# A sandwich transformer block on one core: output projection with doubled adapter and y buffers, low parts ahead of statistics, inverses made early, two pieces moved behind attention

## The reference

```python
x = x + layernorm(attn(layernorm(x)))
x = x + layernorm(ffn(layernorm(x)))
```

## Time and profile before

| | us |
|---|---|
| median of the runs (3) | 1255.57 |
| lowest and highest | 1255.46, 1257.33 |
| the profiled execution's own time | 1251.13 |
| its span, first to last instruction | 1249.4 |
| TensorE busy in the span | 1111.8 (89%) |
| DVE busy | 708.5 (57%) |
| ACT busy | 493.9 (40%) |
| POOL busy | 249.8 (20%) |
| mean granted clock of TensorE | 0.934 of full |

### The profile page before, as it was taken

The page is one execution under the profiler, slowest core; times in us unless marked ns, Lnnn a source line. Parts: engine busy times, 40 slices in busy tenths (PEclk is TensorE's granted clock), DMA queues, the critical chain, the costliest instruction groups (busy, mean ns, idle before and its releaser), DMA issues. The chain is left out here.

```text
span 1249.4 us, 18070 instructions
## 1 busy us (share of the span) xinstructions
PE 1111.8 (89%) x7020; PEld 760.4 (61%) x7020; DVE 708.5 (57%) x983; ACT 493.9 (40%) x1042; POOL 249.8 (20%) x251
## 2 busy tenths in 40 slices
PE   3999999889999999999998975455999999999996
PEld 1877778534455555555553443344888888887884
DVE  4756747777787878877887353354433324324213
ACT  3233233246677777777776431111321111111110
POOL 3525438101311112111111222231000001001001
PEclk9999999687999999999998788676999999999998
DMA  6356686544434445555440433453210200200100
GB/s 238 97 142 176 158 183 172 104 104 78 78 79 79 79 78 101 93 92 95 87 124 24 126 101 109 136 152 118 63 43 1 101 1 9 93 1 17 51 1 34
DMA packets 93417, 113.08 MB, mean 91 GB/s; under 512 B 26260, under 2 KB 54036, under 8 KB 93332
## 3 DMA queue, kind: packets, MB, share of 16 engines
q1 hardware_dynamic: 91476, 108.21, 34.0%
q10 hardware_dynamic: 1856, 3.71, 1.7%
HBM read 68.83 MB, written 42.21 MB: 89 GB/s over the span
## 5 line engine op out<-in xcount | busy, mean ns | idle before, releaser
L828 ACT ACTIVATE prob<-ps_s 128x512 f32<-128x512 f32 (+3 forms) x768 | 323.9, 496 | 185.4 <-PE ps_s L974 178.5
L850 DVE TENSOR_REDUCE neg<-ps_m 128x2 f32<-128x1024 f32 (+2 forms) x224 | 248.2, 1145 | 56.1 <-PE ps_m L939 36.2
L974 PE MATMUL ps_s<-q_op,k_op 50*128 50x512 f32 (+2 forms) x768 | 242.5, 449 | 17.8 <-ACT prob L828 13.2
L939 PE MATMUL ps_m<-k_op,q_op 48*128 48x512 f32 (+2 forms) x768 | 183.5, 416 | 10.5 <-DVE neg L850 6.8
L974 PEld LDWEIGHTS ps_s<-q_op,k_op 50*128 50x128 f32 x768 | 117.5, 192 | 121.5 <-ACT prob L828 60.4
L787 POOL TENSOR_SCALAR_AFFINE_SELECT prob<-prob 128x512 f32<-128x512 f32 x128 | 81.3, 636 | 409.7 <-ACT prob L828 409.7
L988 PE MATMUL ps_y<-prob,vg 128*17 128x512 f32 (+3 forms) x1536 | 153.2, 520 | 0.0
L1504 DVE TENSOR_TENSOR hf<-sl,ps_u 128x512 f32<-128x512 f32 (+1 forms) x44 | 30.2, 687 | 192.0 <-PE ps_u L78 165.5
L850 DVE TENSOR_REDUCE neg_far<-ps_m 128x4 f32<-128x512 f32 (+2 forms) x96 | 100.0, 1048 | 30.1 <-PE ps_m L944 28.6
L1569 PE MATMUL ps_d<-w_high,wp_high 128*128 128x512 f32 (+1 forms) x352 | 115.0, 389 | 0.0
L939 PEld LDWEIGHTS ps_m<-k_op,q_op 48*128 48x128 f32 x768 | 95.9, 196 | 29.0 <-DVE neg L850 20.0
(11 more groups left out here) (164 smaller groups left out, 1683.9 us busy)
## 6 DMA issues: line engine op xcount, KB each, us to landing
y_heads<-y_sb SPq DMA_DIRECT2D x32, 256.0 KB, 2.1
raw<-in_w_ffn SPq DMA_DIRECT2D x31, 256.0 KB, 4.8
k_op<-k_parts SPq DMA_DIRECT2D x28, 256.0 KB, 4.4
q_op<-q_parts SPq DMA_DIRECT2D x56, 128.0 KB, 5.0
v_groups<-v_out SPq DMA_DIRECT2D x16, 272.0 KB, 4.1
x<-in_x SPq DMA_DIRECT2D x4, 1024.0 KB, 7.8
q_parts<-part_h SPq DMA_DIRECT2D x16, 256.0 KB, 2.9
q_parts<-part_l SPq DMA_DIRECT2D x16, 256.0 KB, 2.9
```

What stands on the lines that cost most here:

```text
L828: act.activation(prob[:, v % NPROB, h, unit_cols(u)], ps_s[:, y % NS, unit_cols(u)], ACT.Exp, scale=D ** -0.5).then_inc(s_exp, 1)
L850: nc.vector.tensor_reduce(to[:, :, pairs[0]:pairs[-1] + 1, i - TT * c], scores, axis=AX.X, op=ALU.max, negate=True).then_inc(a_read, 1)
L939: last = nc.tensor.matmul(ps_m[:, g % 2, s, base:base + wide], q_op[buf][r, c, pair, (i - TT * c) * P:(i - TT * c + 1) * P], k_op[buf][r, ...
L974: nc.tensor.matmul(ps_s[:, y % NS, lo:BLK], k_op[buf][r, pair, j * P:(j + 1) * P], q_op[buf][r, c, pair, lo:BLK], start=True, stop=True)\
```

## The change

- The sums are loaded in four DMAs by 256 columns, into a tile of 128 rows; batch 0's in iteration 11 of SP's loop (before: 13), and their inversion stands on DVE behind the last maximum of group 12 (before: behind the last of all). place_inverses(0) moves to iteration 13 (before: end of 14). For batch 1, 28 heads' sums are loaded in iteration 15 and the last four heads' are copied straight out of y_sb.
- ya gets a second buffer, and y a pair of its own for pieces 4 and 5 (y_late).
- In attention, spreads 0 to 2 and projects 0 and 1 stand in earlier slots; project(2) leaves the slots and stands behind attention's last product, and project(3) behind spread(5). finish(1) comes ahead of low(2), finish(2) moves behind attention.
- In stage_project, low(m + 2) and divide(m + 3) come between finish(m) and finish(m + 1). The feed-forward tiles 12 to 19 are split in the feed-forward stage, now three a slice (tiles 12 to 15 are still loaded before), and its first transposes stand beside project(6).
- Feed-forward's PSUM banks are exchanged (ps_g, ps_u with ps_f), and ACT's waits at its start are put at tile 22.

The diff, cut to its core:

```diff
--- before.py
+++ after.py
@@ -37,8 +37,8 @@
+NPB = NP // B
...
-LATE_WEIGHTS = 20
@@ -725,21 +725,26 @@
+            if n == NG - 5:
+                for c in range(HB):
+                    sp.wait_ge(y_out[c], 16 * NHG)
+                tail.load_sums(sp, 0, H)
             if n == NG - 3:
...
-                for c in range(HB):
-                    sp.wait_ge(y_out[c], 16 * NHG)
-                tail.load_sums(sp, 0)
+                tail.place_inverses(sp, 0)
                 tail.load_y(sp, 0)
...
             if n == NG - 1:
+                for c in range(HB):
+                    sp.wait_ge(y_out[c], 16 * (NG - 1))
+                tail.load_sums(sp, 1, H - HG)
                 for i in range(8, 12):
                     tail.load_weights(sp, i)
-                tail.load_ya(sp, 2)
+                tail.load_ya(sp, 3)
                 tail.load_y(sp, 3)
@@ -749,16 +754,18 @@
             if n == NG - 2:
-                tail.place_inverses(sp, 0)
+                sp.wait_ge(pv, NU * (NG - 2))
+                tail.load_ya(sp, 1)
                 for i in range(4, 8):
                     tail.load_weights(sp, i)
-                tail.load_ya(sp, 1)
+                tail.load_ya(sp, 2)
                 tail.load_y(sp, 2)
+        tail.copy_sums(sp, y_sb, 0)
         tail.store_x1(sp, 1)
         tail.load_x(sp, 2)
-        tail.load_ya(sp, 3)
+        tail.load_ya(sp, 4)
         store_y(NG - 1, 1)
-        tail.store_x1(sp, 2)
+        tail.copy_sums(sp, y_sb, 1)
@@ -786,19 +793,19 @@
+                if (n, u) == (NG - 2, 8):
+                    tail.add_adapter(pool, 0)
                 if (n, u) == (NG - 2, 10):
-                    tail.add_adapter(pool, 0)
-                if (n, u) == (NG - 2, 11):
                     tail.add_adapter(pool, 1)
-                if (n, u) == (NG - 1, 3):
+                if (n, u) == (NG - 1, 2):
                     tail.inverse_deviation(pool, 0)
                     tail.residual_pool(pool, 0)
+                if (n, u) == (NG - 1, 3):
                     tail.add_adapter(pool, 2)
                     tail.inverse_deviation(pool, 1)
                     tail.residual_pool(pool, 1)
+                if (n, u) == (NG - 1, 8):
                     tail.add_adapter(pool, 3)
-        tail.inverse_deviation(pool, 2)
-        tail.residual_pool(pool, 2)
@@ -808,7 +815,7 @@
-        highs = {(NG - 2, 11): 0, (NG - 1, 2): 1, (NG - 1, 7): 2, (NG - 1, 10): 3}
+        highs = {(NG - 2, 10): 0, (NG - 1, 0): 1, (NG - 1, 6): 2, (NG - 1, 10): 3}
@@ -886,7 +893,8 @@
-        tail.invert(dve, 0)
+                if entry == (NG - 4, NK - 1):
+                    tail.invert(dve, 0)
@@ -899,22 +907,22 @@
-        weights(NG - 4, range(4))
+        weights(NG - 4, range(2))
+        tail.divide(dve, 0)
+        weights(NG - 4, range(2, 4))
+        tail.divide(dve, 1)
         weights(NG - 3, range(4, 6))
-        tail.divide(dve, 0)
+        tail.low(dve, 0)
         weights(NG - 3, range(6, 8))
-        tail.divide(dve, 1)
-        tail.low(dve, 0)
         tail.low(dve, 1)
         finish(0)
         tail.divide(dve, 2)
         weights(NG - 2, range(8, 10))
+        finish(1)
         tail.low(dve, 2)
-        finish(1)
         tail.divide(dve, 3)
         weights(NG - 2, range(10, 12))
         tail.low(dve, 3)
-        finish(2)
@@ -1011,8 +1019,8 @@
-        for step, m, slot, parts in ((tail.spread, 0, 5, 2), (tail.spread, 1, 8, 2), (tail.project, 0, 14, 4), (tail.spread, 2, 18, 2),
-                                     (tail.project, 1, 20, 4), (tail.spread, 3, 24, 2), (tail.project, 2, 27, 4)):
+        for step, m, slot, parts in ((tail.spread, 0, 2, 2), (tail.spread, 1, 6, 2), (tail.project, 0, 11, 4),
+                                     (tail.spread, 2, 15, 2), (tail.project, 1, 19, 4), (tail.spread, 3, 24, 2)):
...
@@ -1064,14 +1072,16 @@
-            y_in*2 yad_in xr_in over_ps y_div y_sum y_high y_low o_ps
+            y_in*4 yad_in*2 xr_in over_ps y_div y_sum y_high y_low o_ps
...
-        self.y, self.ya, self.xr = room.put("y", [P, 2, CC, W]), room.put("ya_sb", [P, CC, W]), room.put("xr", [P, PT, C])
+        self.y, self.xr = room.put("y", [P, 2, CC, W]), room.put("xr", [P, PT, C])
+        self.ya = [room.put("ya_sb0", [P, CC, W]), nc.alloc_sbuf_tensor_at("ya_sb1", [P, CC, W], F32, offset=start["vg0"])]
+        self.y_late = nc.alloc_sbuf_tensor_at("y_late", [P, 2, CC, W], F32, offset=start["qr"])
@@ -1091,19 +1101,25 @@
+    def y_of(self, m):
...
+        return (self.y_late if m in (NPB, NPB + 1) else self.y)[:, m % 2]
     def load_y(self, sp, m):
+        b, at = m // NPB, slice(m % NPB * W, (m % NPB + 1) * W)
+        if m in (2, 3):
...
+        elif m >= NPB + 2:
+            sp.wait_ge(self.y_low, m - 3)
...
-            sp.dma_start(self.y[:, m % 2, c], self.d["y_heads"][heads_c, 0:D, at]).then_inc(self.y_in[m % 2], 16)
+            sp.dma_start(self.y_of(m)[:, c], self.d["y_heads"][heads_c, 0:D, at]).then_inc(self.y_in[m % NPB], 16)
     def load_ya(self, sp, m):
-        if m:
-            sp.wait_ge(self.y_sum, m)
-        sp.dma_start(self.ya[:], self.d["ya"][b, :, :, at]).then_inc(self.ya_in, 16)
+        b, at = m // NPB, slice(m % NPB * W, (m % NPB + 1) * W)
+        if m >= 2:
+            sp.wait_ge(self.y_sum, m - 1)
+        sp.dma_start(self.ya[m % 2][:], self.d["ya"][b, :, :, at]).then_inc(self.ya_in[m % 2], 16)
@@ -1127,31 +1143,37 @@
-    def load_sums(self, sp, b):
-        if b:
-            sp.wait_ge(self.inv_in, 16 * HB * b)
-        sp.dma_start(self.sums[:], self.d["y_heads"][b * H:(b + 1) * H, D].rearrange("h (k t) -> k h t", k=HB))\
-            .then_inc(self.sums_in, 16)
+    def load_sums(self, sp, b, heads):
...
+        src = self.d["y_heads"][b * H:b * H + heads, D].rearrange("h (k t) -> k h t", k=NPB)
+        for k in range(NPB):
+            sp.dma_start(self.sums[k * H:k * H + heads, b], src[k]).then_inc(self.sums_in, 16)
...
+    def copy_sums(self, sp, y_sb, c):
...
+        for k in range(2):
+            row = (2 * c + k) * H + H - HG
+            sp.dma_start(self.sums[row:row + HG, B - 1], y_sb[D:P:32, c, k * W:(k + 1) * W]).then_inc(self.sums_in, 16)
...
-        for k in range(HB):
-            cols = slice((b * HB + k) * BLK, (b * HB + k + 1) * BLK)
-            sp.dma_start(self.inv[0:H, cols], self.sums[k * H:(k + 1) * H]).then_inc(self.inv_in, 16)
+        for k in range(NPB):
+            sp.dma_start(self.inv[0:H, (b * NPB + k) * W:(b * NPB + k + 1) * W], self.sums[k * H:(k + 1) * H, b])\
+                .then_inc(self.inv_in, 16)
     def invert(self, dve, b):
-        dve.wait_ge(self.sums_in, 16 * (b + 1))
-        self.nc.vector.reciprocal(self.sums[:], self.sums[:]).then_inc(self.inverse, 1)
+        dve.wait_ge(self.sums_in, 16 * (NPB if b == 0 else 3 * NPB))
+        self.nc.vector.reciprocal(self.sums[:, b], self.sums[:, b]).then_inc(self.inverse, 1)
     def divide(self, dve, m):
-        dve.wait_ge(self.y_in[m % 2], 16 * CC * (m // 2 + 1))
+        dve.wait_ge(self.y_in[m % NPB], 16 * CC * (m // NPB + 1))
...
-        self.nc.vector.tensor_tensor(self.y[:, m % 2], self.y[:, m % 2], self.ps_r(m), op=ALU.mult).then_inc(self.y_div, 1)
+        self.nc.vector.tensor_tensor(self.y_of(m), self.y_of(m), self.ps_r(m), op=ALU.mult).then_inc(self.y_div, 1)
...
-        self.nc.vector.tensor_tensor(self.y_l[:, m % 2], self.y[:, m % 2], self.y_h[:, m % 2].bitcast(F32),
+        self.nc.vector.tensor_tensor(self.y_l[:, m % 2], self.y_of(m), self.y_h[:, m % 2].bitcast(F32),
...
@@ -1259,104 +1281,114 @@
         tail.load_y(sp, 4)
-        tail.load_sums(sp, 1)
-        tail.load_x(sp, 3)
         tail.load_y(sp, 5)
-        tail.load_ya(sp, 4)
-        tail.place_inverses(sp, 1)
-        tail.store_x1(sp, 3)
-        tail.load_x(sp, 4)
-        tail.load_weights(sp, 12)
-        tail.load_weights(sp, 13)
         for half in range(2):
             sp.wait_ge(tail.x1_out[half], 16)
         sp.dma_start(tail.x1_first[:], tail.d["x1_blocks"][0]).then_inc(tail.x1_in, 16)
-        for m in last_m:
-            if m + 1 < NP:
-                tail.load_ya(sp, m + 1)
...
+        tail.load_y(sp, 6)
+        tail.load_ya(sp, 5)
+        tail.place_inverses(sp, 1)
+        tail.load_y(sp, 7)
+        for i in range(EARLY_WEIGHTS, EARLY_WEIGHTS + 4):
+            tail.load_weights(sp, i)
+        for m in range(2, NP):
             tail.store_x1(sp, m)
             if m + 1 < NP:
                 tail.load_x(sp, m + 1)
+            if m < NPB:
+                tail.load_ya(sp, m + 4)
     def _(pool):
-        tail.inverse_deviation(pool, 3)
-        tail.add_adapter(pool, 4)
-        tail.residual_pool(pool, 3)
-        for m in last_m:
-            if m + 1 < NP:
-                tail.add_adapter(pool, m + 1)
-            if m == NP - 2:
-                tail.f_inverse_deviation(pool, 0)
+        def finish(m):
...
+        finish(2)
+        tail.add_adapter(pool, 4)
+        tail.add_adapter(pool, 5)
```

(99 more changed lines are left out.)

36 lines of the change are left out of this document (14 added, 22 removed).

## The result

The changed kernel takes 1223.91 us (median of 4 runs, 1219.34 to 1227.31), the kernel before on the same chip 1255.51: ratio 0.9745, 95% interval 0.971 to 0.978. A second comparison of the same kernel (e7) gave 0.9751. It is 32 us faster; 53 were forecast, and 1223.91 lies outside the range of 1191 to 1221. Its profiled execution has a span of 1221.0 us, 28.4 less than before.

The account below looks back on a forecast made before the run. TensorE was taken to bound attention and feed-forward, with a chain of waits between. The terms +7.8 - 13.1 - 46.4 - 1.2 = -52.9 us, from the median 1255.6, gave 1202.7; range 1191 to 1221.

Parts of the forecast that it names:

- Part 5: Feed-forward: splitting eight more tiles there costs 0, less low clock at its start gives -1.2 us.
- A: Rival, 0.13: in attention the sums land as on a free queue, 1199.7; also distance, group 12's last maximum to maxima's end.
- Part 1: Early inversion in attention: DVE waits for the sums, TensorE stands 5.8 us, then low clock 2.0: +7.8 us, bounds +3 and +10.
- D: Rival, 0.04: after the stop TensorE's low clock stays through attention, up to +77, net +19: 1275.
- Part 2: Attention's last two groups: waits and project(2) leave, a wait at project(0) comes: -13.1 us, bounds -17 and -6.
- Part 3: From attention's last result copied (E) to the spreads: they start at E + 16.6, before 20.8; bounds 15.6 and 20.5.
- Part 4: Pieces from the spreads to feed-forward, DVE as the chain: feed-forward starts at E + 60, before 106.4.
- the forecast's case: Whole kernel: the parts as forecast, terms off by a few us, 1202.7; chance 0.62; projects 4 to 7 start 7 to 9 apart.
- B: Rival, 0.11: behind attention pieces keep a pitch of 16, 1233; also distance, maxima's end to attention's last result copied.
- C: Rival, 0.08: feed-forward starved by weight loads, +6, 1209; also distance, attention's last result copied to first spread.

Follow-up runs that it names:

- e7: The changed kernel again, without an edit: ratio 0.9751 to the kernel before.
- e3: Changed kernel with project(0) one slot later in attention, and spread(2) with it: ratio 0.9693 to the kernel before.
- e4: Changed kernel with SP placing batch 1's inverses ahead of x1_first, y of 6 and ya of 5: ratio 0.9651 to the kernel before.
- e9: Changed kernel with low(5) to low(7) each behind the finish of the piece ahead, as before the change: ratio 0.9894 to the kernel before.
- e6: e5's kernel with DVE adding both halves of the residual for pieces 3 to 5 and POOL none: ratio 0.957 to the kernel before.
- e2: Changed kernel with SP issuing the sums' loads ahead of group 14's load, inversion left in place: ratio 0.9643 to the kernel before.
- e5: Changed kernel with e3's and e4's edits and batch 0's inversion moved behind group 13's last maximum: ratio 0.9554 to the kernel before.

## Why the prediction was right, and why it was wrong

The direction was right, and so were the mechanism of each part in the main and the place of the waits for the sums, for low(0) and for the spreads. The collision of DVE with POOL was not foreseen. The size was not right: four terms were too favourable, by 6.0, 9.4, 6.0 and 4.1 us in parts 1 to 4; with 0.4 in Part 5, less the 1.5 that lie ahead of A, that is the difference between the 52.9 forecast and the 28.4 of the profiled execution.

**Part 1: +7.8 forecast, 13.8 measured (12.6 in e7).** The landing (595.0 forecast, 594.08 measured) and the stop (5.8 and 5.82) were right, and so was the rule of the ring order that stood beside them. The step that failed is "half of that is lost: 2.4, of which I take 2.0": it carried the one return to full speed that it had read, 4.9 us behind a wait in front of a project, over to attention as a fixed price. There the return took 3.8 to 12.2 us of nearly unbroken work in five traces with the same stop, and what lies beyond the stop itself cost 8.0 us here and 6.0, 3.8, 1.9 and 4.1 in e7, e3, e4 and e9. So 2.0 was the smallest of what came, met in one trace of five. The row that was nearest had been in hand: 0.60 over 12 us with TensorE busy for 10.5, used for rival D and not for this term. By 12 us at that row's clock the term would have been near 5, and the part 10.5, which is what the first trace had lost when its clock was back; the further 3.3 are the two short falls at 653 and 673.

**Part 2: -13.1 forecast, -3.7 measured (-6.1 in e7).** The waits of 3.35 and 6.45 us and project(2) did leave. The steps that failed: "TensorE waits 3.2" at project(0) is 4.57, since low(0) takes 3.12 us beside POOL's adapter sum and not 1.21 (e3 takes the wait down to 1.87); and "I add 1" for the low clock. The spreads were moved into the 15 us at 0.50 behind the maxima, and project(2)'s 5.5 and 2.0 us were counted as if each us of matmul taken out were a us won. The windows show them missing: TensorE is busy for 0.7 us more than before in this stretch and not for 7.5 less, and all that was won is idle time (14.2 us before, 9.4 here). e3 brings the part to -8.2, and 5 us of the forecast stay away; I made no run that takes the low clock out of this stretch, so its share in them is argued and not shown.

**Part 3: spreads at E + 16.6 forecast, E + 22.6 measured (20.9).** The step that failed is "some 3 MB of loads are queued ahead of it now, for which I add 1", with a landing of 2.2. It was 7.0, the issues took 3.43 us and not 2.4, and they began at E + 12.1 and not 11.0. The bound I named, a landing of 7.1, gave 20.5 and is near what came; I had applied the ring's rule to Part 1 at its full price and to the same kind of DMA here with 1 us only. e4 shows it: the same DMAs ahead of the bulk give E + 13.2.

**Part 4: 43.4 us from the spreads to feed-forward forecast, 47.5 measured.** The order of events was right: project(4) 12.7 us behind the first spread (12.0 forecast), project(6) after 32.6 (28.7), project(7) after 42.0 (37.4), with DVE as the chain. The pieces start 7.1, 12.7 and 9.4 us apart, where 7 to 9 were to show the forecast's case. What was missing is the collision with POOL: low(5) and low(6) 1.1 us each and f_normalize 2.1, 4.3 in all ahead of project(6), whose lag is 3.9. The durations of low and of f_normalize had been read where none of POOL's large adds ran beside them. e6 tests the part of the low parts: with 0.6 us of added work in each piece it still gives 1.1 us.

**Part 5** was right: -1.2 forecast, -0.8 measured.

**The rivals.** A (the sums land as on a free queue) is false, DVE waited; e2 makes it true by exchanging two lines, and that is worth more than A's 3 us, because in that trace the clock then stays up. B is false: projects 4 to 7 take 34.8 us and not four pitches of 16; e9 shows what keeps the pitch away. C is false (380.6). D is false in its "without end", but its mechanism, a low clock that attention's matmuls take long to leave, was the one that missed the most in Part 1; between 5 us and never there was no case in the forecast. Its price doesn't come out of its own terms either: 77 us less the forecast's 52.9, with the 2.0 not counted twice, is +22 and not +19; and what stood against it, that every project of before got back to full speed within 5 us, has an exception in project(6), where it took 5.5 (833.33 to 838.8). **The range** took the bounds of parts 1 to 3 from each one's nearest row and left 18 us upwards. Added up they come to 13.2 us upwards and 9.7 down, not to "about 8 us either way"; three of these bounds (+10, -6, 20.5) were passed together (in the first trace). With the three causes taken away, e5's 0.9554 of 1255.6 is 1199.6, near the forecast's 1202.7, but that is luck too: its A is 6.6 us and its C 4.3 below the forecast, its B 5.1 and its D 4.3 above.

## What to carry to other kernels

Put small DMAs that someone waits for ahead of the bulk in their queue, at both ends of a stage: two exchanges of order were worth about 12 us (e2) and 7 to 10 (e4). A stop of TensorE can be paid twice, once idle and once in the clock. Price the return of the clock as a range from several rows, not from one (here 1.9 to 8.0 us lost beyond the same stop), and an instruction of DVE by one that has POOL working beside it. When a chain has two engines in turn, pull the part that the other engine waits for (low) ahead of the part that only closes the piece (finish).

## What I had not expected of the hardware

- TensorE's return to full clock took 3.8 to 12.2 us of nearly unbroken work behind the same stop of about 6 us, in the same stretch of attention (five traces, 3.8 in e4 and 12.2 in the changed kernel's). In a project it was 4.9 us. A stop of 0.9 us was followed by a fall of about 10 us in three of eight traces.
- The clock also fell for 3 to 4 us with TensorE busy throughout, at other places in each trace of one kernel (653 and 673 in the changed kernel's, 619 in e7's).
- DVE's low part takes 1.22 us alone and 2.3 beside POOL's add of 128x512 (1.8 us), 3.12 beside POOL's add of 128x1024 (2.34 us, begun 0.3 us earlier); it ends about 1.1 us after POOL in each case.
- The issue of the same four DMAs on SP took 2.50 us in e4 and 3.43 us behind six more DMAs (x1_first, y of 6, ya of 5).
